# Edge attributes of a graph network: transposed into the sums' PSUM banks, copied out by VectorE

## The reference

```
# layer 0: attention over relations, 4 heads
e     = leaky_relu(el + er)                       # one number an edge and head
alpha = exp(e - max) / segment_sum(exp(e - max))  # over the edges of one destination
h     = segment_sum(alpha * feat[type, src], dst)
# layer 2: edge network and three dense layers
e   = relu(edge_attr @ ee_w1 + ee_b1) @ ee_w2 + ee_b2    # 64 -> 256 -> 256
agg = segment_sum(x[src] + e, dst)
```

## Time and profile before

| | us |
|---|---|
| median of three timed runs | 3268.11 (3263.8 to 3269.29) |
| span of the profiled execution | 3494.0 |
| busy: TensorE / VectorE / ScalarE / GpSimd | 2934.6 / 1869.1 / 1260.7 / 1013.3 |
| edge loop in the profile: first and last add on VectorE | 551.7, 1658.1 |
| first gather, last scatter on GpSimd (starts) | 466.2, 1763.5 |

### The profile page before, as it was taken

How to read it: one execution, slowest core, us unless ns; L and a number is a source line. 1 busy time by engine, 2 the same in 40 slices (tenths; PEclk the granted TensorE clock), 3 DMA queues, 4 the chain that set the end, 5 groups by cost and what they waited for, 6 DMA issues and landing times.

```text
span 3494.0 us, 48240 instructions
## 1 busy us (share of the span) xinstructions
PE 2934.6 (84%) x15020; PEld 1947.6 (56%) x15084; DVE 1869.1 (53%) x5320; ACT 1260.7 (36%) x3665; POOL 1013.3 (29%) x1048
## 2 busy tenths in 40 slices
PE   2799936888888888889268799989999999999998
PEld 2444416777777777778142444445555555545545
DVE  6578745666666665556250543334555555532334
ACT  1122235666666666668020220004444444420000
POOL 2144465666666666665710000000000000000000
PEclk6699968898999899999559699999999999999999
DMA  8966643222222222221128243330000000022232
GB/s 250 363 180 194 183 125 86 70 73 74 71 74 71 73 74 72 74 66 28 31 71 301 82 119 103 101 118 6 3 6 6 6 3 6 23 76 79 78 101 80
DMA packets 245032, 314.35 MB, mean 90 GB/s; under 512 B 121467, under 2 KB 168484, under 8 KB 240740
## 3 DMA queue, kind: packets, MB, share of 16 engines
q1 hardware_dynamic: 191412, 175.79, 17.8%
q0 software_dynamic: 49104, 104.11, 10.2%
q10 hardware_dynamic: 4320, 31.95, 2.3%
HBM read 234.14 MB, written 77.59 MB: 89 GB/s over the span
## 4 chain that ended last, share of the span: by engine, by line
PE 57%; DVE 15%; issue 11%; ACT 7%; another core or an unknown queue 4%; DVEq 3%; DMA 3%; SPq 0%; ACTq 0%
PE PS L1153 15%; PE PS L998 14%; PE PS L964 7%; PE PS L939 5%; PE PS L977 5%; PE PS L822 4%; ACT BG L653 3%; DMA BG<-a_d 3%; DVE BG L1703 2%; DVEq L1582 2%; DVE OHB L1430 1%; ACT SL L736 1%; DVE AL L1790 1%; DVE SUMS L1411 1%
## 5 line engine op out<-in xcount | busy, mean ns | idle before, releaser
L1567 DVE TENSOR_TENSOR SUMS<-SUMS,PS 128x640 f32 x500 | 409.2, 818 | 374.2 <-PE PS L939 220.7
L532 POOL DMA_INDIRECT BG<-feat_d,IDXST x500 | 485.9, 972 | 337.9 <-PE PS L939 157.4
L523 POOL DMA_INDIRECT a_d<-VAL,IDXS x499 | 492.3, 987 | 314.3 <-DVE VAL L1424 133.2
L1153 PE MATMUL PS<-BG,SL 128*128 128x512 f32 (+1 forms) x1440 | 539.1, 530 | 12.0 <-ACT SL L736 12.0
L653 ACT ACTIVATE BG<-BG,SL 128x64 f32<-128x64 f32 x2000 | 513.4, 336 | 0.0
L1153 PEld LDWEIGHTS PS<-BG,SL 128*128 128x128 f32 x1440 | 277.0, 195 | 251.7 <-issue 222.4
L564 POOL MEMSET BG<- 128x7680 f32 x1 | 6.5, 6501 | 1327.3 <-DVE MV L1834 1327.3
L964 PE MATMUL PS<-W1A,X 65*128 65x256 f32 x1000 | 295.2, 421 | 81.8 <-ACT X L627 60.4
L939 PE MATMUL PS<-OHB,BG 128*128 128x128 f32 x2000 | 357.2, 305 | 0.2
L977 PE MATMUL PS<-OHB,X 128*128 128x128 f32 x2000 | 337.5, 295 | 23.1 <-issue 22.6
L977 PEld LDWEIGHTS PS<-OHB,X 128*128 128x128 f32 x2000 | 306.7, 208 | 40.0 <-issue 25.1
(11 more groups left out here) (298 smaller groups left out, 4093.0 us busy)
## 6 DMA issues: line engine op xcount, KB each, us to landing
BG<-a_d SPq DMA_DIRECT2D x171, 256.0 KB, 4.2
AL<-a_d SPq DMA_DIRECT2D x137, 256.0 KB, 2.6
a_d<-BG POOLq DMA_DIRECT2D x30, 1088.0 KB, 40.2
feat_d<-SUMS ACTq DMA_DIRECT2D x30, 1040.0 KB
BG<-rel_d SPq DMA_DIRECT2D x100, 160.0 KB
X<-in_edge_attr_dram SPq DMA_DIRECT2D x124, 128.0 KB
SUMS<-a_d SPq DMA_DIRECT2D x52, 256.0 KB, 2.6
SL<-key_d SPq DMA_DIRECT2D x50, 192.0 KB
```

The source lines that it names most:

```text
L523: pool.indirect_dma_start(a_d.rearrange("n (w o) -> (n w) o", o=1), bass.IndirectOffsetOnAxis(ap=IDXS[:, t:t + 1], axis=0), VAL[:, t:t + 1 ...
L532: pool.indirect_dma_start(RING[:, t // NB % 3, t % NB, :], None, feat_d.rearrange("n (r d) -> (n r) d", r=R), bass.IndirectOffsetOnAxis(ap ...
L1153: last = pe.matmul(PS[:, to + q, 0:width], lhs[:, i, c, :], w[:, c, q * width:(q + 1) * width], start=(c == 0), stop=(c == kc - 1))
L1567: add = tt(a, a, SUM_AT[n % 3].rearrange("p (a n) -> p a n", a=5), ALU.add)
```

## The change

For groups 2 to 124 the transposes go into the unused columns 768 to 1023 of the pair of banks that block n uses (`TURN_AT[n % 3]`), no longer into bank 6. They are issued between the block's `hidden_sum` and its `gat_sum` and no longer behind the latter, and wait for the attributes' load alone. VectorE copies them out in two pieces (`net_turned`), behind its wait for the block's `gat_sum` and ahead of the block's add. ScalarE keeps `edge_turned` for groups 0 and 1 only. `hidden` waits for the copies of its own group before its first half, where it waited for those of the next group before its second.

```diff
+        TURN_AT = [PSF[:, 1024 * i + 6 * P:1024 * i + 8 * P] for i in range(3)]
...
             def edge_turned(v):
                 act.wait_ge(s("ea_used"), v + 1)
-                if v >= 2:
-                    act.wait_ge(s("hid_ps"), 2 * (v - 1))
...
-                    if k % 4 == 3 and v + 2 < NE:
-                        edge_turned(v + 2)
...
-            def net_turn(v):
+            def net_turn(v, to):
...
-                if v >= 2:
-                    pe.wait_ge(s("hid_ready"), 2 * (v - 1) + 1)
                 for k in range(2):
-                    last = turn(EDGE_TURN[:, k * P:(k + 1) * P],
+                    last = turn(to[:, k * P:(k + 1) * P],
...
             def hidden(v, q):
-                if v == 0 or q == 1:
-                    pe.wait_ge(s("ea_t"), 2 * min(v + 2, NE))
+                if q == 0:
+                    pe.wait_ge(s("ea_t"), 2 * max(v + 1, 2))
...
                     hidden_sum(n)
+                    if k % 4 == 1 and n // 4 + 2 < NE:
+                        net_turn(n // 4 + 2, TURN_AT[n % 3])
                     gat_sum(b, k)
-                    if k % 4 == 1 and n // 4 + 2 < NE:
-                        net_turn(n // 4 + 2)
...
+            def net_turned(v, turned):
+                turned = turned.rearrange("p (k n) -> p k n", k=2)
+                cp(EAT[v % 2][0:ED, 0::2, :], turned[0:ED, :, :]).then_inc(s("ea_t"), 1)
+                cp(EAT[v % 2][0:ED, 1::2, :], turned[ED:2 * ED, :, :]).then_inc(s("ea_t"), 1)
...
                     dve.wait_ge(s("agg_ps"), n + 21)
+                    if k % 4 == 1 and n // 4 + 2 < NE:
+                        net_turned(n // 4 + 2, TURN_AT[n % 3])
```

More of the change, by code:

```diff
@@ L980, in _ @@
             pe.wait_ge(s("dve_mark"), DVE_MARKS["edge_start"])
-            net_turn(0)
-            net_turn(1)
+            net_turn(0, EDGE_TURN)
+            net_turn(1, EDGE_TURN)
             for q in range(2):
```

## The result

The changed kernel takes 3327.85 us (3321.84 to 3339.34), the kernel before 3268.70 in the same session: a ratio of 1.0194, 95% interval 1.0176 to 1.0211. It is 59 us slower, where 3265 was forecast and the range ended at 3292.

The account below looks back on a forecast made before the run. It took GpSimd's indirect DMAs to bound the timed runs, so TensorE's 30 us stayed hidden; 1.5 us from early gathers and 1.5 from waits for blocks made 3 us less, 3265 us, range 3232 to 3292.

Parts of the forecast that it names:

- GpSimd as the bound of the kernel before: Edge loop: GpSimd's 849 indirect DMAs from block 26 to the adjacency bound the timed runs, its scatters ending at 1565 us.
- computed floor: Whole kernel: GpSimd's stream alone allows a total of 3248 us; the median lies 20 us above that.
- the faster rival: Edge loop: GpSimd has slack in timed runs, so 10 to 35 us come through, about 3248 us; chance 0.23.
- The late releases: Edge loop and behind it: late ends of waits belong to the profiled execution only, explaining its 226 us over the median.
- The transposes' wait: TensorE in the edge loop: no more waiting for hidden values or ScalarE, 1.2 us a batch, 30 us in all.
- ScalarE's copies: ScalarE in the edge loop: 246 copies of 0.370 and 0.380 us go, 92 us, worth nothing alone.
- VectorE's copies: VectorE in the edge loop: gains 246 copies from PSUM at 0.42 us, 4.2 us in 20 blocks.
- It fits, with nothing to spare: VectorE in the 350 counted blocks: 35 us of work per 20 blocks against TensorE's 36.0 now, 34.8 after.
- The slower rival: Edge loop at k = 10: VectorE becomes the bound, 3287 us, or 3306 if TensorE gains nothing; chance 0.20.
- 39.0 us a batch: Counted batch if VectorE is the bound: 36.0 - 1.2 + 4.2 us, against GpSimd's share of 37.8.
- five such places: Each batch: all five pairs of VectorE copies fall where VectorE needs 5.6 us against TensorE's 5.4 for three blocks.
- TensorE's hidden sum three blocks later: Edge loop: this sum waits for the add behind each pair of VectorE's copies, so lateness would reach TensorE there.

Follow-up runs that it names:

- no_copies_half: Changed kernel without VectorE's 246 copies (attributes of groups 0 and 1 read repeatedly) and with 172 of 349 later scatters left out: 3173.9 us, ratio 0.9731.
- before_half: Kernel before with 172 of the 349 scatters in and behind the loop left out: 3164.3 us, ratio 0.9688.
- no_copies: Changed kernel without VectorE's 246 copies, transposes still made in their new place, attributes of groups 0 and 1 read repeatedly: 3275.6 us, ratio 1.0035.
- copies_off_run: Changed kernel without VectorE's copies at k = 5 and 9 of a batch, those at 1, 13 and 17 kept: 3264.5 us, ratio 0.9992.
- copies_in_run: Changed kernel with VectorE's copies at k = 5 and 9 alone, without those at 1, 13 and 17: 3318.1 us, ratio 1.0159.
- halved kernels: Kernel before and changed kernel, each with 172 of the 349 later scatters left out: 3164.3 and 3262.2 us.
- before_iota: Kernel before with the one-hot's constant read from PSUM and the one-hots put between the wait for a block's sum and its add: 3253.0 us, ratio 0.996.
- before_moved: Kernel before with the one-hots put between the wait for a block's sum and its add, constant still read from SBUF: 3266.8 us, ratio 1.0008.
- late_exp: Changed kernel with ScalarE's soft_exp moved from k = 12 to 15 and TensorE's soft_back from 14 to 15: 3284.3 us, ratio 1.006.

## Why the prediction was wrong

*GpSimd as the bound of the kernel before: right.* Its last scatter starts at 1564.4 us where the working gave 1565, and taking load off GpSimd, 220 us or 15, shortens the kernel. One term was small: from the last scatter to the first product 6 us were assumed, and it is 22.7, since that scatter takes long to land (the chain of waits, kernel before profiled again):

```profile
1564.42 17.95 DMA a_d<-VAL,IDXS
```

That is most of the 20 us that the median lay above the computed floor. They were no slack, so the faster rival built on them fell.

*The late releases: right.* They were in none of the later profiles.

*The transposes' wait and ScalarE's copies.* The 1.2 us a batch were three times too much for quiet counted batches, 0.4 us (35.6 in no_copies_half, 36.0 in before_half), and near for those without counts, 1.5. As predicted they moved nothing (no_copies). But it was not GpSimd alone that kept them from showing: with half of the scatters left out no_copies_half is slower than before_half, 3173.9 against 3164.3 us, since TensorE still waits at block 12 and its clock falls behind that.

*VectorE's copies.* The price was right, 0.413 and 0.426 us for 0.42. The step that failed is the next: "It fits, with nothing to spare", by which the copies cost nothing. It was a mean over 20 blocks, 35 us of work in 36. But VectorE's work isn't spread evenly: it runs without a pause longer than 0.15 us from the start of a batch to the end of `soft_shift`, and has its idle time behind k = 10. The two pairs of copies at k = 5 and 9, 1.7 us, put it off by 1.5: it ends 4.39 us after the sum of block 9 in copies_off_run, 5.93 with them. Nothing in the stretch can take them up, and TensorE's wait at block 12 grows with it, from 25.5 us to 61.8 (34.0 in no_copies, so that most of the growth is the copies').

*The slower rival.* It had the right place, k = 10, and nearly the right price, 39.0 us a batch against 38.6 in batches without the slow clock; but it came to that price by other terms, so that is luck. Three things were wrong. It saw five such places in a batch where the runs show two: k = 10, and k = 2, where the copies of k = 1 put off `soft_in` and TensorE's `soft_turn` waits for it (21.3 us; none in copies_in_run). And it let the lateness reach TensorE through "TensorE's hidden sum three blocks later", for which 6.3 us were waited; the main way is ScalarE's `soft_exp`, which stands in ScalarE's order ahead of weights that do not depend on it. That way was in the first profile already, from 600 to 1400 us, and the prediction didn't follow it:

```profile
PE PS L937 <- ACT BG L653: 12.7, 12, 2.1
```

Then the rival left out the slow clock that follows such a wait. Per counted batch the loss is 38.6 - 35.9 = 2.7 us without it, and the waits from 560 to 1510 us give the same: (61.8 - 25.5) / 23 = 1.6 us more for the weights, 0.9 for `soft_turn`, 0.3 for the hidden sums. The slow clock adds 41.7 - 38.6 = 3.1. That it does so shows in counted batches with the same wait of 2.9 us in the changed kernel's trace: they take 38.6 to 38.8 us where the clock stays at 1.00, 40.3 to 40.7 with 3.4 us at 0.50, about 41.5 with 6.8, and 45.0 to 45.4 with 13.7. Wait and clock come to 99 us over 17 batches. The halved kernels, where GpSimd isn't the bound, differ by 98, of which 82 lie in these batches (17 x 4.8) and most of the rest in the last seven; that the two sums are so near is chance. What GpSimd covers is the difference between the 98 and the 59 measured, 39 us. No run had the wait without the clock or the clock without the wait: their shares are worked out from the lengths of the batches.

The Trainium skill's advice that the prediction set against this change (Perfetto Trace Analysis, section Optimizing Scalar/DVE Operations: offload from VectorE when it is saturated) was right here in direction. Its difference between the engines is not what cost the time: 246 copies at 0.413 and 0.426 against 0.370 and 0.380 us are 11 us, and by themselves the copies at three places of five cost nothing.

What stays open: why the granted clock falls for 13.7 us in one batch, for 3.4 in another and not at all in a third, behind waits of the same length.

## What to carry to other kernels

A mean over a period says whether an engine can keep up, not whether it does: find the stretch in which it never pauses, and add to it nothing on which another engine waits in order. When a wait is small and stands at a fixed place of every period, it marks where added work can come through nearly in full. And before moving work off an engine, ask by its busy pitch which engine is the bound: here GpSimd, busy for 31% of the span, and neither end of the move touched it.

## What the runs showed of the hardware

An indirect DMA on GpSimd that starts while VectorE runs a one-hot comparison is held until that is over. The kernel before, VectorE's line and then GpSimd's:

```profile
790.01 0.82 DVE L1526 TENSOR_TENSOR OHB<-IOTA,DREL 128x640 f32<-128x640 f32 x1
```

```profile
790.37 1.30 POOL L532 DMA_INDIRECT BG<-feat_d,IDXST  x1 [0.30 <-issue]
```

0.46 us of the one-hot were left when the gather started, and it took 1.30 us in place of 0.95. Over the 71 such transfers of the loop the length is what is left of the one-hot plus 0.82 us on average, 1.16 us in the mean; one that starts during an add of the running sums takes 0.96. The one-hot reads both its operands from SBUF, the add one from PSUM. With the constant in PSUM (before_iota) GpSimd does 552 transfers from 600 to 1300 us in place of 545:

```profile
L533 POOL DMA_INDIRECT BG<-feat_d,IDXST x368 | 353.4, 960 | 112.1 <-issue 87.7 <-PE PS L940 24.4
L524 POOL DMA_INDIRECT a_d<-VAL,IDXS x184 | 180.0, 978 | 56.1 <-issue 56.1
```

The Trainium skill says (SBUF — State Buffer, section Who interferes with whom) that a VectorE instruction with two inputs in SBUF contends with a GpSimd instruction that reads SBUF. The trace agrees, 1.16 us against 0.96. The same section infers that a `tensor_tensor` does not hold up the making of a DMA's descriptors; this one-hot is a `tensor_tensor`, and the gather was held to 1.30 us all the same, though no run shows which part of it waited. before_iota against before_moved gives the effect a price, 13 us of a kernel that GpSimd bounds. It is also where most of the 10 to 18 us that late_exp and no_copies lose lies, although GpSimd waits for nothing there: about as many of its transfers start inside a one-hot, but earlier in it, and they take 1.38 and 1.31 us in the mean. The transfers over 1.1 us were together 22 us longer than their median before, and 37 and 35 us in these two.

The other thing is the clock: a wait of 2.9 us on TensorE was followed by up to 13.7 us at 0.50 granted, and such a batch took 45.0 to 45.4 us in place of 38.6, over twice the wait.
